# Scores of three units ahead of a row's last down product, and each softmax V product in one piece of 512 columns

## The reference

```python
xn = layernorm(x)
# attention 1: causal, 1 - tanh(e)^2 in place of a softmax
e    = (where(causal, -10000, q @ k.T * scale) - phase_threshold) / tau
attn = 1 - tanh(e) ** 2
s    = (attn / (attn.sum(-1) + 1e-6)) @ v @ Wo.T
# attention 2: a full softmax, then a router and nine SwiGLU networks of width 256
h    = rmsnorm(xn) * norm1_w
X    = xn + softmax(q2 @ k2.T * scale) @ v2 @ wo
h2   = rmsnorm(X) * norm2_w
comb = softmax over the two best of 8 of softmax(h2 @ router_w)
Y    = X + swiglu(h2, shared) + sum_e comb[e] * swiglu(h2, expert e)
out  = x + s * silu(Y)
```

## Time and profile before

| | us |
|---|---|
| median of 3 runs | 1149.21 |
| lowest and highest of them | 1147.17, 1158.49 |
| the profiled execution, its own time | 1157.05 |
| its span, first to last instruction | 1155.2 |
| busy: TensorE, VectorE, ScalarE, GpSimd | 1032.3, 856.3, 652.9, 347.4 |
| mean granted clock of TensorE, share of full | 0.97 |

### The profile page before, as it was taken

One profiled execution on the slowest core, in us unless ns is written; L12 is line 12 of the kernel. 1 busy time (PEld: TensorE's weight loads), 2 busy tenths in 40 slices (PEclk: granted clock), 3 DMA queues, 4 the chain that ended last, 5 costly groups with the idle time before them and its releaser, 6 DMA issues.

```text
span 1155.2 us, 18598 instructions
## 1 busy us (share of the span) xinstructions
PE 1032.3 (89%) x6912; PEld 471.8 (41%) x6912; DVE 856.3 (74%) x1716; ACT 652.9 (57%) x888; POOL 347.4 (30%) x194
## 2 busy tenths in 40 slices
PE   3459999989999999999999899999999889999998
PEld 1102355324652346423554245522465235542364
DVE  7447687759977597786877589775986869774872
ACT  4027862588326972378624884269723786248831
POOL 6500335103630154303352035400552033520023
PEclk9558999999999999999999999999999999999999
DMA  5540225103441045201251024310342113500020
GB/s 176 117 54 2 49 68 132 34 2 77 109 68 29 3 96 127 38 20 44 64 141 25 11 63 122 69 28 2 96 116 41 30 29 69 148 9 20 1 75 9
DMA packets 71785, 69.65 MB, mean 60 GB/s; under 512 B 8528, under 2 KB 63056, under 8 KB 71568
## 3 DMA queue, kind: packets, MB, share of 16 engines
q1 hardware_dynamic: 68928, 64.41, 24.7%
q10 hardware_dynamic: 2768, 4.06, 1.0%
HBM read 53.37 MB, written 14.81 MB: 59 GB/s over the span
## 4 chain that ended last, share of the span: by engine, by line
PE 56%; DVE 21%; ACT 11%; DMA 4%; issue 3%; SPq 3%; POOL 1%; ACTq 0%; DVEq 0%; POOLq 0%
PE O L1019 9%; PE O L1035 8%; DVE nmax L677 7%; DVE PT L714 7%; ACT PT L554 6%; PE S L1051 6%; PE S L1053 5%; PE S L994 5%; PE S L1052 5%; PE M L963 4%; PE M L960 4%; PE M L946 2%; DVE PT L840 2%; SPq L337 2%; SPq L327 1%
## 5 line engine op out<-in xcount | busy, mean ns | idle before, releaser
L554 ACT ACTIVATE PT<-S 128x1024 f32<-128x1024 f32 (+1 forms) x448 | 420.7, 971 | 117.3 <-PE S L994 115.0
L677 DVE TENSOR_REDUCE nmax<-M 128x1 f32<-128x512 f32 x512 | 330.6, 685 | 119.4 <-PE M L960 80.4
L714 DVE SCALAR_TENSOR_TENSOR PT<-PT 128x768 f32<-128x768 f32 (+1 forms) x192 | 215.6, 1171 | 96.4 <-ACT PT L554 96.0
L1019 PE MATMUL O<-PT,V 128*12 128x256 f32 (+3 forms) x2816 | 242.2, 424 | 0.0
L423 POOL TENSOR_TENSOR split<-split,parts 128x512 f32<-128x512 f32 x32 | 91.0, 2844 | 433.2 <-ACT parts L514 433.2
L438 POOL TENSOR_TENSOR PT<-PT,CB 128x1024 f32<-128x1024 f32 x56 | 133.2, 2385 | 278.0 <-DMA CB<-scrC 158.2
L588 ACT ACTIVATE PT<-S 128x1024 f32<-128x1024 f32 x72 | 73.9, 1027 | 250.7 <-PE S L1053 250.6
L994 PE MATMUL S<-stackQ,stackK 64*128 64x512 bf16 (+3 forms) x1024 | 192.1, 347 | 21.6 <-DMA stackQ<-mTZ 8.4
L1051 PE MATMUL S<-h2hi,wgu_hi 128*128 128x512 f32 x288 | 150.5, 522 | 0.1
L1035 PE MATMUL O<-PT,wdn 128*128 128x512 f32 x288 | 142.7, 595 | 0.0
L960 PE MATMUL M<-KX,stackQ 128*128 128x512 bf16 x256 | 104.3, 409 | 28.5 <-DMA KX<-scrK 21.3
(11 more groups left out here) (189 smaller groups left out, 1042.5 us busy)
## 6 DMA issues: line engine op xcount, KB each, us to landing
CB<-scrC SPq DMA_DIRECT2D x64, 256.0 KB, 5.7
stackQ<-scrQ SPq DMA_DIRECT2D x192, 64.0 KB
stackK<-scrK SPq DMA_DIRECT2D x192, 64.0 KB
scrQ<-parts SPq DMA_DIRECT2D x16, 384.0 KB, 5.0
scrK<-parts SPq DMA_DIRECT2D x16, 384.0 KB, 7.8
KX<-scrK SPq DMA_DIRECT2D x96, 32.0 KB
PT<-in_w_gu ACTq DMA_DIRECT2D x2, 1152.0 KB, 8.0
xin<-in_x SPq DMA_DIRECT2D x8, 256.0 KB, 2.9
```

What stands on the lines that cost most here:

```text
L554: a.activation(PT[:, n % SLOTS, 2 * q * w:2 * q * w + 2 * w].rearrange("p (r n) -> p r n", r=2), S[k][:, :].rearrange("p (r n) -> p r n", ...
L677: v.tensor_reduce(nmax[:, h % 2, h // 2, t:t + 1], M[k][:, :], AX.X, ALU.max, negate=True).then_inc(m_read[k], 1)
L714: v.scalar_tensor_tensor(p, p, 1.0, p, ALU.subtract, ALU.mult).then_inc(weighed, 1)
L1019: last = t_.matmul(O[k][32 * q:32 * q + VW, i0:i1], V[:, j, 4 * g + q, :], PT[:, n % SLOTS, w * q + at:w * q + at + i1 - i0], start=(j == ...
```

## The change

1. The scores and exponentials of unit 2 of the next batch row move ahead of the last down product (`SEAM = 3`; `second_scores`, `third_scores`): TensorE issues them between the residual and down product 8, with the maxima of list 1 between the two pairs. The tanh (`gate`) moves behind unit 3's first exponential, the product with S behind list 2, the gated product behind list 3.
2. The slot of unit n becomes (n + 3) % 4, so that units 0, 1 and 2 use slots 3, 0 and 1; the waits on down products and on V follow from it.
3. V of a stage-1 unit moves from unit n + 2 to unit n + 3, whole, between the unit's two pairs of scores (in unit 3 behind the second pair). Unit 17 takes V of units 14 and 15, whole.
4. The maxima of Y are distributed anew: 2, 2, 6 and 6 in lists 0, 1, 3 and 4 (1, 3, 4, 4, 4 in lists 0 to 4 before), those of Z 4, 4, 4, 4 (3, 4, 4, 5). `outT` moves from list 3 to list 4.
5. ScalarE's copies of O for groups 0 to 2 stand in units 7, 11 and 15 (6, 10 and 14 before).

```diff
@@ -43,6 +43,12 @@
 SLOTS = 4
+SEAM = 3
+
+
+def slot(n):
+
+    return (n + SLOTS - 1) % SLOTS
@@ -67,9 +73,9 @@
-spread(MAX["Y"], {0: 1, 1: 3, 2: 4, 3: 4, 4: 4})
-spread(MAX["Z"], {5: 3, 6: 4, 7: 4, 8: 5})
-PLACES[3].insert(2, "outT")
+spread(MAX["Y"], {0: 2, 1: 2, 3: 6, 4: 6})
+spread(MAX["Z"], {5: 4, 6: 4, 7: 4, 8: 4})
+PLACES[4].insert(3, "outT")
 PLACES[5].insert(2, "maxT_Y")
@@ -546,22 +552,29 @@
                     act.wait_ge(pv_done, it * UNITS + n + 1)
-                done = {0: 0, 1: 1, 2: DEPTH}
+                done = {1: 0, 2: 1, 3: DEPTH}
                 if q == 0 and n in done and it * DOWNS + done[n] > 0:
                 act.wait_ge(s_full[k], c + 1)
-                a.activation(PT[:, n % SLOTS, 2 * q * w:2 * q * w + 2 * w].rearrange("p (r n) -> p r n", r=2),
+                a.activation(PT[:, slot(n), 2 * q * w:2 * q * w + 2 * w].rearrange("p (r n) -> p r n", r=2),
                              S[k][:, :].rearrange("p (r n) -> p r n", r=2)[:, :, 0:w],
+            def gate(it):
+
+                act.wait_ge(out_scaled, it + 1)
+                a.activation(gT[:, :], O[0][:, :], ACT.Tanh, scale=0.5).then_inc(o_read[0], 1)
+
             def row(u, it, following):
                 bt = it + 1
-                outs = {**{NT * G + NT + (2 if G < NG - 1 else 1): G for G in range(NG)}, **{N1 + 3 * g + 6: NG + g for g in range(NG - 2)},
+                outs = {**{NT * G + NT + (3 if G < NG - 1 else 1): G for G in range(NG)}, **{N1 + 3 * g + 6: NG + g for g in range(NG - 2)},
                         UNITS - 1: 2 * NG - 2}
-                for n in range(2, UNITS):
+                for n in range(SEAM, UNITS):
                     names = u.places[n]
                     weights(it, n, 0)
+                    if n == SEAM and it > 0:
+                        gate(it - 1)
                     for name in names[:len(names) // 2]:
@@ -584,7 +597,7 @@
                     if e < DEPTH:
-                        act.wait_ge(pv_done, it * UNITS + UNITS + e + 1)
+                        act.wait_ge(pv_done, it * UNITS + UNITS + e + 2)
                     a.activation(AB[e % DEPTH], S[k][:, :], ACT.Silu).then_inc(s_read[k], 1)
@@ -595,13 +608,13 @@
                     a.activation(warm[:, :], n1s[:, :], ACT.Exp)
-                    for q in range(2):
-                        weights(it + 1, 0, q)
-                    take(u, "maxT_W", bt)
-                    for q in range(2):
-                        weights(it + 1, 1, q)
-                act.wait_ge(out_scaled, it + 1)
-                a.activation(gT[:, :], O[0][:, :], ACT.Tanh, scale=0.5).then_inc(o_read[0], 1)
+                    for n in range(SEAM):
+                        for q in range(2):
+                            weights(it + 1, n, q)
+                        if n == 0:
+                            take(u, "maxT_W", bt)
+                else:
+                    gate(it)
@@ -618,7 +631,7 @@
                             a.activation(wgu_hi[:, :, i * F:i * F + F], gu_raw[i], ACT.Copy).then_inc(gu_hi, 1)
-            for n in range(2):
+            for n in range(SEAM):
                 for q in range(2):
@@ -710,7 +723,7 @@
                 w = width(n)
-                p = PT[:, n % SLOTS, 2 * q * w:2 * q * w + 2 * w]
+                p = PT[:, slot(n), 2 * q * w:2 * q * w + 2 * w]
                 v.scalar_tensor_tensor(p, p, 1.0, p, ALU.subtract, ALU.mult).then_inc(weighed, 1)
@@ -797,9 +810,9 @@
                         take(u, it, name)
-                    if n == 0 and it > 0:
+                    if n == SEAM - 1 and it > 0:
                         out_by_s(it - 1)
-                    if n == 1 and it > 0:
+                    if n == SEAM and it > 0:
                         out_gated(it - 1)
@@ -1017,7 +1030,7 @@
                         last = t_.matmul(O[k][32 * q:32 * q + VW, i0:i1], V[:, j, 4 * g + q, :],
-                                         PT[:, n % SLOTS, w * q + at:w * q + at + i1 - i0],
+                                         PT[:, slot(n), w * q + at:w * q + at + i1 - i0],
                                          start=(j == 0), stop=(NT - 1 in js and j == js[-1] and half != 0))
@@ -1146,11 +1159,23 @@
-            def row(u, it, following):
-                v_at = {n: n - 2 for n in range(2, N1 + 2)} | {n: n - 3 for n in range(N1 + 3, UNITS)}
+            def second_scores(u, it):
+
+                for q in range(2):
+                    scores(it, 1, q)
+                for name in u.places[0]:
+                    work(u, it, name)
+
+            def third_scores(u, it):
+
+                scores(it, 2, 0)
                 for name in u.places[1]:
                     work(u, it, name)
-                for n in range(2, UNITS):
+                scores(it, 2, 1)
+
+            def row(u, it, following):
+                v_at = {n: n - 3 for n in range(SEAM, UNITS) if n not in (N1 + 1, N1 + 2)}
+                for n in range(SEAM, UNITS):
                     if n == N1 - 1:
@@ -1163,9 +1188,9 @@
                             scores(it, n, i // 2)
-                        elif v_at.get(n, N1) < N1 and v_at[n] % NT > 0:
-                            with_v(it, v_at[n], i // 2)
-                        elif n in v_at and i == 1:
+                        elif n == N1 + 1:
+                            with_v(it, N1 - 2 + i // 2)
+                        elif n in v_at and i == (3 if n == SEAM else 1):
                             with_v(it, v_at[n])
@@ -1185,13 +1210,12 @@
                     work(u, it, "maxT_W")
-                    for q in range(2):
-                        scores(it + 1, 1, q)
-                    for name in ROWS[it + 1].places[0]:
-                        work(ROWS[it + 1], it + 1, name)
+                    second_scores(ROWS[it + 1], it + 1)
                 for t in range(NT):
                 last.then_inc(down_done, 1)
+                if following:
+                    third_scores(ROWS[it + 1], it + 1)
                 for _step in second_product(it, NE - 1):
@@ -1205,10 +1229,8 @@
             first_scores(0)
-            for q in range(2):
-                scores(0, 1, q)
-            for name in ROWS[0].places[0]:
-                work(ROWS[0], 0, name)
+            second_scores(ROWS[0], 0)
+            third_scores(ROWS[0], 0)
             for it in range(B):
```

## The result

| | before | after | ratio (95% interval) |
|---|---|---|---|
| first measurement, median | 1153.18 us (4 runs, 1147.17 to 1158.49) | 1170.34 us (4 runs, 1165.97 to 1178.29) | 1.0146 (1.0103 to 1.0188) |
| repeated later | 1155.61 us (23 runs) | 1167.21 us (5 runs, 1163.82 to 1169.27) | 1.0105 (1.0063 to 1.0147) |
| profiled execution (span) | 1157.05 us | 1178.29 us (1176.6) | |

The changed kernel is slower by 1 to 1.5%. The forecast had the sign and the mechanism; the time, 1170.34, is 9.1 above the forecast 1161.2 and 2.3 above the upper end of the range, 1168. The repeat's 1167.21 lies inside the range, by 0.8. The profiled execution is the slowest of the first four.

What follows compares the result with a forecast made beforehand. Bound: TensorE and VectorE passing maxima through two PSUM buffers, then ScalarE's exponentials. 0.85 + 0.35 + 0.4 = 1.6 us a row, 11.2 for rows 1 to 7, plus 0.8, on 1149.2 gave 1161.2 us; range 1141 to 1168.

Steps and rivals of the forecast that it cites:

- The loop: Units 6 to 8: whole V, two reductions and a refill of two PSUM buffers take 3.07 us, against 2.64 with halves.
- 0.85 later: End of stage 1's first regime: unit 9's scores start 0.85 us later in a row than before.
- The walk: Step-by-step timing of the two maxima buffers from the seam through units 3 to 8, up to unit 9's scores.
- V between unit 9's pairs, 0.35: Unit 9: whole V (0.98 instead of 0.55) delays the second score pair, so ScalarE starts 0.35 us later.
- A tie, nothing added: Unit 12: scores released by the transfer of Z's maxima at 519.1, ScalarE arriving at 519.6, so no added wait.
- Q2, 0.4: Start of stage 2: two whole V products in unit 17 delay projection Q2, and ScalarE's split of it by 0.4 us.
- Row 0, 0.8: First row: only the later part of the 0.85 applies; 0.8 us slower, estimated between 0 and 2.5.
- its own bounds: Units 3 and 4 and the tanh, without a twin in the trace: from 2.4 us earlier to 1.5 later.
- rival 1: VectorE stays fed and the head start comes through: 1.6 us a row faster, 13 in all, 1136 us; chance 0.2.
- 1 and 2: rival 1, and a second, a draw: the 0.85 vanishes, 0 to 0.8 us a row slower, 1153 us; chance 0.25.
- Rival 3: Tanh behind unit 3's first exponential delays V of unit 0: 16 to 19 us slower, 1167 us; chance 0.1.
- Rival 4: The change does not do what it says; no size or chance given.

Runs made afterwards that it cites:

- e2: The kernel before with every V product whole, still two units ahead, maxima and seam unchanged; 1173.55 us, 1.0145 of before.
- e5: The changed kernel with each maximum's reduction over 256 of its 512 columns; 1139.09 us (one run).
- e4: The changed kernel with V in halves in units 4 to 8, whole from unit 9, and V14 in unit 16; 1169.22 us, 1.0115 of before.
- e1: The changed kernel with V in halves again in units 4 to 15, except the first of each group; 1168.71 us, no ratio given.
- e3: The changed kernel with V14 moved to unit 16 instead of beside V15 in unit 17; 1166.65 us, 1.0095 of before.
- a2: The changed kernel measured again, unchanged, on a later occasion; 1167.21 us, 1.0105 of before.
- b2: The kernel before measured again, unchanged, on a later occasion; 1155.45 us, 0.9996 of before.
- f2: The changed kernel with each maximum's matmul of units 3 and 4 issued twice (the fill); 1192.36 us, 1.0383 of before.
- f3: e4's kernel with halves up to unit 15 and each maximum's matmul of units 3 and 4 issued twice; 1161.89 us, 1.0070 of before.
- f1: e4's kernel with each maximum's matmul of units 3 and 4 issued twice; 1166.88 us, 1.0110 of before.
- g2: The changed kernel with maxima spread evenly over units 3 to 8, V whole; 1170.19 us, 1.0125 of before.
- g1: The changed kernel with maxima spread evenly over units 3 to 8, V in halves, V14 in unit 16; 1158.04 us, 1.0016 of before.

## Why the prediction was right and wrong

- **The loop: right.** 3.07 between V starts as forecast, 0.56 idle on TensorE, 0.58 on VectorE (forecast 0.6); e2 shows it without the other part, e5 with another reduction.
- **Unit 9's scores "0.85 later": over.** They came 26.68 after unit 1's (519.02 - 492.34), forecast 27.1, before 26.2: 0.46. The walk put unit 3's scores at 5.04 after unit 1's; they came at 4.74. The second maximum ahead of the residual was sized at 0.32 and cost 0.02 (the residual starts 493.10 - 492.34 = 0.76 after unit 1's scores, 0.74 before); of the steps behind it, scores and maxima took 0.2 less than sized, the residual and the down product 0.2 more. That 0.3, and 0.1 more in unit 4, ran through to unit 9.
- **V between unit 9's pairs, 0.35: right.** The transposed maxima left ScalarE 2.16 after unit 9's first exponential (521.88 - 519.72), before 1.82: 0.34.
- **"A tie, nothing added" at unit 12: wrong.** ScalarE waited 0.15 and 0.22 there, and 13.04 instead of 12.70 passed from the transposed maxima to the load: 0.34. e4 has the same 13.03 and e1 12.70, so it is V whole, not the head start; e2, two units ahead, has 12.93 (536.80 - 523.87).
- **Q2, 0.4: right,** 0.48; e3 takes it away alone.
- **A row: 1.6 forecast, 0.46 + 0.34 + 0.34 + 0.48 = 1.62 measured.** The table load was said to stand 42.6 after unit 1's scores, and stood at 42.58. Two errors of 0.3 to 0.4 cancelled, which is luck. Whole undisturbed rows (1 to 6) came out 1.5 longer, since stage 2 gave a little back. The sum also gave the last row a wait for Q2, which that row does not have; a2's last row was still 2.0 longer than b2's (131.90 against 129.91).
- **Row 0, 0.8: too small.** Its table load came 1.88 later in the first pair of profiles (44.73 against 42.85) and 2.3 in the second (43.43 against 41.14), and Q2 adds 0.49: 2.4 to 2.8. The estimate took the late part of the 0.85 only, and left out the 0.34, 0.34 and 0.48, which row 0 pays like any other; and up to its table load row 0 has a mean clock of 0.83 to 0.90 in these four profiles, so that its V and its matmuls can take longer than those on which the terms were sized (no run separates that part). The end of the bounds, 2.5, was the better value.
- **"It stands 0.7% above the median, so the forecast goes on the median": the step that missed the range.** With 1157.05 as a base the same sum gave 1169, and that was set aside for 1149.2, a median of three runs. The four medians of before on four occasions were 1153.18, 1156.02, 1153.37 and 1155.61, the last of 23 runs. 1155.6 + 12.0 is 1167.6; a2 measured 1167.21. Of the 9.1 us missed, 4 are in the base (1153.18 - 1149.21) and 1.5 to 2 in row 0. All nine runs of after together have the median 1167.21, inside the range, so that the miss also hangs on which four runs were taken.
- **What is left, some 3 us, is of the size of a dip.** The range had no term for stretches at half clock, since the profile of before has none ahead of the table loads of its rows 1 to 7. The profile of after has one, 5.2 us, and that of e1 three, 13 us. No run separates their share in the medians of after from the spread of runs.
- **The range was narrower than its own bounds.** The prediction allowed 1.5 more in a row for units 3 and 4 and the tanh, up to 12 us in eight rows, and ended the range 7 us above the forecast. At its lower end half of rival 1's gain of 13 is 1142.7, not 1141.
- **Rivals.** 1 and 2 fell with the 3.07. Rival 3: the tanh ended at 498.52 + 0.59 = 499.11, and V of unit 0 started at 499.45, so it was not late, though by 0.34 only. Rival 4: both parts did as they say.

The Trainium skill, Perfetto Trace Analysis, section Optimizing Scalar/DVE Operations, advises breaking up instructions of ScalarE and VectorE that cause bubbles on other engines. The prediction carried that over to TensorE, for which the page does not state it, and held it against the merging. Here it came out right: a split V loses 0.12 on TensorE and gains 0.43 in the loop.

**What stays open.** Most dips of the kernels with three units ahead begin 13.6 to 18 us after a row's first exponential, behind units 3 and 4. Of the profiles with six maxima in each of these units and no fill, after, e1, e3 and e4 had dips there, a2 and e5 none; with the fill f2 and f3 had, f1 none; evenly spread, g2 had none, and g1 one, 26.5 us after the first exponential. Others begin elsewhere: in after, f1, f2 and g2 in the last row, behind its table load, and in e5 and b2 some 35.5 us after it, behind unit 12's wait for the transfer of Z's maxima. TensorE's timeline in e5, and the 4 us before the clock fell:

```profile
907.07 0.39 PE L1007 MATMUL S<-stackQ,stackK 64*128 64x512 bf16 x2 [2.57 <-DMA stackQ<-mTZ]
```

```profile
904.20:908.20 4.00, 1.43 (x12) 0.22 (x10) 1.84 (x8) 2.49 (x4) 0.00 (x0) 1.00 0.01 3
```

So some come behind a single long wait (1.55 in b2, 2.57 in e5), and those behind units 3 and 4 while TensorE never idles for 0.6 at a time. For these, the Trainium skill, TensorE: Matmul & The Clock Gate, section A second HAM failure mode: psum-queue depth-cycling, describes a clock that goes to and fro where TensorE idles briefly and often between groups of matmuls. e1 and e4, with the most idle time there, fit, and so does f1 against e4; f2 does not, and rows 3 and 5 of after did the same work with different ends. What a dip comes to is shown, 1.2 to 5.3 us; why it comes in one row and not in the next is not.

## What to carry to other kernels

An operation that stands between a producer and the consumer of a two-buffer ring sets the ring's period by its length; before merging two halves, add up the loop (the long operation, the latency to the reader, the reads of what is buffered, the refill), since 0.12 us saved on the busiest engine cost 0.43 here. The head start of one unit was worth 0.5 of some 135 us a row here, and nothing once the maxima were spread evenly. And before a sum is set on a base, look at how many runs that base has and at the granted clock beside each: a median of three was 4 to 7 us below the later ones, where the change cost 12 to 17.

## What the runs showed that was not expected

- The granted clock falls to 1.2 GHz in the midst of work and stays there for 3.4 to 17 us. In after, e1, e3 and f2 TensorE was idle less than 0.6 us at a time in the 4 us before it. In e1 one run took 1150.38 us at a mean clock of 0.974, another 1171.59 at 0.948.
- More work on TensorE in the idle places raised the clock in one kernel (f1) and lowered it in another (f2).
- The first table load comes at 73.5 to 82.8 us after the start of the span in these profiles, whatever the kernel, so two profiles can differ by 9 us before the first row begins. Distances within a row mostly repeat to 0.03 us where neither the clock nor the transfer of Z's maxima disturbs them: compare those. That transfer alone put the table load back by 0.9 us in row 4 of before.
